# First attention's loop in double steps, with the V transposes in psX and evicted by VectorE

## The reference, cut to what matters

```python
q = (query @ Wq).reshape(b, sq, 32, 16).transpose(0, 2, 1, 3)
k = (key @ Wk).reshape(b, sk, 8, 16).transpose(0, 2, 1, 3)
v = (value @ Wv).reshape(b, sk, 8, 16).transpose(0, 2, 1, 3)
k = jnp.repeat(k, 4, axis=1); v = jnp.repeat(v, 4, axis=1)
scores = jnp.einsum('bhqd,bhkd->bhqk', q, k) * 16 ** (-0.5)
probs = jax.nn.softmax(scores, axis=-1)
out = jnp.einsum('bhqk,bhkd->bhqd', probs, v)
```

## Time and profile before

| what | us |
|---|---|
| median of three runs | 3961.32 |
| span of the profiled execution | 3957.1 |
| the loop `all_batches`, first to last exponential (start) | 104.1 to 1012.1 |
| one batch in the middle of the loop (first maximum unit to the next batch's) | 561.20 to 618.40, 57.20 |
| busy in 561 to 618: TensorE / VectorE / ScalarE / GpSimd | 56.50 / 37.92 / 33.00 / 25.42 |

### The profile page before, as it was taken

One profiled execution on the slowest core, in us unless ns is written; L12 is line 12 of the kernel. 1 busy time (PEld: TensorE's weight loads), 2 busy tenths in 40 slices (PEclk: granted clock), 3 DMA queues, 4 the chain that ended last, 5 costly groups with the idle time before them and its releaser, 6 DMA issues. The chain is left out here.

```text
span 3957.1 us, 74929 instructions
## 1 busy us (share of the span) xinstructions
PE 3617.3 (91%) x32220; PEld 2431.4 (61%) x32220; DVE 2263.6 (57%) x2562; ACT 1538.2 (39%) x2218; POOL 1386.7 (35%) x892
## 2 busy tenths in 40 slices
PE   6999999999768689999999999999999998686888
PEld 4555555555233456887777788887878746333334
DVE  4666666666279832444544444444444416698972
ACT  2555555555177312222222222222222203676740
POOL 3344444431089311111111111111111004497971
PEclk8999999999789889999999999999999999798999
DMA  6455555552223042111111111111111112221220
GB/s 206 127 139 146 143 141 138 152 133 70 67 78 92 1 157 79 40 39 30 47 31 48 31 40 48 40 48 40 48 40 44 71 41 53 73 91 59 95 66 22
DMA packets 229009, 302.18 MB, mean 76 GB/s; under 512 B 68560, under 2 KB 174992, under 8 KB 227392
## 3 DMA queue, kind: packets, MB, share of 16 engines
q1 hardware_dynamic: 228680, 297.40, 25.6%
HBM read 243.77 MB, written 53.10 MB: 75 GB/s over the span
## 5 line engine op out<-in xcount | busy, mean ns | idle before, releaser
L1754 POOL TENSOR_TENSOR D_ctx_lo<-D_ctx_raw,D_ctx_hi 128x1904 fp32r<-128x1904 f32 x64 | 254.7, 3980 | 1294.2 <-ACT D_ctx_hi L1748 1294.2
L762 DVE TENSOR_REDUCE A_mxc<-A_psX 128x2 f32<-128x768 f32 (+2 forms) x512 | 485.5, 984 | 207.5 <-PE A_psX L792 206.5
L1058 ACT ACTIVATE A_probs<-A_psE 128x1024 f32<-128x1024 f32 (+1 forms) x416 | 426.2, 1025 | 318.5 <-PE A_psE L1091 313.4
L1772 ACT ACTIVATE D_V<-D_psY 119x384 f32<-119x384 f32 x224 | 109.8, 490 | 843.0 <-PE D_psY L1839 843.0
L2096 ACT ACTIVATE D_probs<-D_psE 119x2048 f32<-119x2048 f32 x112 | 210.5, 1879 | 414.9 <-PE D_psE L2223 414.9
L1788 DVE TENSOR_REDUCE D_mxc<-D_psE 128x4 f32<-128x1904 f32 (+1 forms) x128 | 242.2, 1892 | 190.8 <-PE D_psE L1858 190.6
L1839 PE MATMUL D_psY<-D_wv_hi,D_ctx_hi 128*119 128x384 f32 (+1 forms) x896 | 314.8, 351 | 16.4 <-DVE D_K_lo L1783 9.0
L2141 DVE TENSOR_TENSOR D_acc<-D_acc,D_probs 119x1024 f32<-119x1024 f32 x96 | 117.6, 1225 | 353.9 <-ACT D_probs L2096 353.9
L2237 PE MATMUL D_psO<-D_probs,D_V 119*32 119x256 f32 (+1 forms) x5376 | 313.3, 381 | 0.0
L1839 PE MATMUL D_psY<-D_wv_hi,D_ctx_lo 128*119 128x384 f32 (+1 forms) x896 | 302.2, 337 | 0.0
L1839 PE MATMUL D_psY<-D_wv_lo,D_ctx_hi 128*119 128x384 f32 (+1 forms) x896 | 301.9, 337 | 0.0
(11 more groups left out here) (366 smaller groups left out, 7770.7 us busy)
## 6 DMA issues: line engine op xcount, KB each, us to landing
D_ctx_raw<-in_ctx SPq DMA_DIRECT2D x48, 952.0 KB, 5.2
A_land<-in_ctx SPq DMA_DIRECT2D x32, 768.0 KB, 5.7
A_land<-in_ctx SPq DMA_DIRECT2D x16, 1024.0 KB, 5.8
E_Bn<-bc_scratch SPq DMA_DIRECT2D x64, 256.0 KB, 3.6
E_Cn<-bc_scratch SPq DMA_DIRECT2D x64, 256.0 KB, 3.4
k_scratch<-A_Khl SPq DMA_DIRECT2D x32, 384.0 KB, 5.4
A_Kst<-k_scratch SPq DMA_DIRECT2D x64, 192.0 KB, 3.6
A_land<-in_ctx SPq DMA_DIRECT2D x16, 642.0 KB, 4.4
```

The source lines that it names most:

```text
L762: nc.vector.tensor_reduce(mxc[:, u % 4, :, u // 4], psX[:, x % 2, :, 0:w], axis=AX_X, op=ALU.max).then_inc(x_free, 1)
L1058: nc.scalar.activation(probs[0:KW[k], n % NPR, :, :].rearrange("p h q -> p (h q)"), psE[0:KW[k], :], ACT.Exp, scale=HD ** -0.5).then_inc(e ...
L1754: nc.gpsimd.tensor_tensor(ctx_lo[c][:, :, 0:w], ctx_raw[c][:, :, 0:w], ctx_hi[c][:, :, 0:w].bitcast(F32), ALU.subtract).then_inc(lo_done[c ...
```

## The change

The loop's unit becomes a double step d (13 in a batch). TensorE's order in one is: scores of the first step, the first maximum unit ("behind"), the weightings of the two steps before (a pair), the other units ("ahead"), scores of the second step, a V transpose if one is due, and one run of 6 or 12 projection passes. At d = 6 the weighting of step 12 stands after the scores of step 13, so that no pair crosses two groups. Other things that move:

- Units are spread three to a double step: those of (j+1, group 0) in d = 6 to 11 (16 = 3+3+3+3+3+1), those of group 1 in d = 12 and d = 0 to 4 of the next batch. `max_rows` comes at d = 5, ahead of the run, and at d = 11, behind it.
- K of chunks 0 and 1 is projected in halves in d = 0 to 3, chunk 2 in d = 4, chunk 3 in d = 5; V of chunks 0 to 2 in halves in d = 6 to 11, chunk 3 in d = 12.
- The V transposes (d = 8, 10, 12, and 0 of the next batch) write psX and take their turn in its two buffers, between the units. VectorE takes them out (`values_out`) in place of ScalarE.
- The reciprocal stands ahead of unit 8 in place of unit 4.
- The queues of SyncE and GpSimd keep their order; what they wait for comes at other times.

```diff
+    RUNS = [("K", 0, HALVES[0]), ("K", 0, HALVES[1]), ("K", 1, HALVES[0]), ("K", 1, HALVES[1]),
+            ("K", 2, range(12)), ("K", 3, range(12)), ("V", 0, HALVES[0]), ("V", 0, HALVES[1]),
+            ("V", 1, HALVES[0]), ("V", 1, HALVES[1]), ("V", 2, HALVES[0]), ("V", 2, HALVES[1]), ("V", 3, range(12))]
+    TURNS = {8: 0, 10: 1, 12: 2, 0: 3}
+    ROWS_FIRST, ROWS_BEHIND = 5, 11
...
+            us = range(min(NU, 3 * max(at, 0)), min(NU, 3 * (at + 1)))
+        units = [("M", b, g, u) for u in us] if b < B else []
+        n = max(1, len(units) // 2)
+        return units[:n], units[n:]
...
+            def values_out(dve, key):
+                b, c = key[1:]
+                x, (t0, nt) = nth_x(key), TILES[c]
+                dve.wait_ge(x_full, x + 1)
+                nc.vector.tensor_copy(V[b % 2][:, t0:t0 + nt, :, 0:HD],
+                                      psX[:, x % 2, 0, 0:P * nt].rearrange("p (j h d) -> p j h d", j=nt, h=H)
+                                      ).then_inc(x_free, 1)
...
+            def turn(pe, key):
+
+                b, c4 = key[1:]
+                x = nth_x(key)
+                pe.wait_ge(y_free, nth_y(("V", b, c4)) + 1)
+                pe.wait_ge(x_free, x - 1)
+                for t in range(TILES[c4][1]):
+                    last = nc.tensor.transpose(psX[:, x % 2, 0, bass.ts(t, P)], VT[:, c4 % 2, bass.ts(t, P)],
+                                               consts["ident"][:, :])
                 last.then_inc(x_full, 1)
...
-                        for n in range(N):
-                            s, k = divmod(n, KT)
-                            to = divmod(s + 1, 2)
-                            units = maxima(k) if to[0] < B else ()
-                            for u in units[:1]:
-                                maximum(pe, *to, u)
-                            scores(n)
-                            for u in units[1:]:
-                                maximum(pe, *to, u)
-                            if n:
-                                weigh(n - 1)
-                            key, passes = projection(s // 2, s % 2, k)
-                            if key:
-                                project(pe, key, passes)
-                            if k == 11 and to[0] < B:
-                                max_rows(pe, *to)
+                        weighed = 0
+                        for j in range(B):
+                            for d in range(TWOS):
+                                n = STEPS * j + 2 * d
+                                behind, ahead = maxima(j, d)
+                                scores(n)
+                                for _, b, g, u in behind:
+                                    maximum(pe, b, g, u)
+                                for e in range(weighed, n):
+                                    weigh(e)
+                                weighed = n
+                                for _, b, g, u in ahead:
+                                    maximum(pe, b, g, u)
+                                scores(n + 1)
+                                if (n + 1) % KT == 0:
+                                    weigh(n)
+                                    weighed = n + 1
+                                if turned(j, d):
+                                    turn(pe, turned(j, d))
+                                if d == ROWS_FIRST:
+                                    max_rows(pe, j, 1)
+                                key, passes = projection(j, d)
+                                if key:
+                                    project(pe, key, passes)
+                                if d == ROWS_BEHIND and j + 1 < B:
+                                    max_rows(pe, j + 1, 0)
+                        weigh(N - 2)
                         weigh(N - 1)
```

More of the change, by code:

```diff
@@ L594, in l0_attention @@
     identr = consts["identr"]
-    K_STEPS = [(0, 3), (3, 3), (6, 3), (9, 3)]
     PASSES = [(c, a, a2) for c in range(DC) for a, a2 in ((0, 0), (0, 1), (1, 0))]
[L598 to L615, removed]
+    TWOS = STEPS // 2
@@ new lines, in l0_attention, with projection @@
+    HALVES = (range(6), range(6, 12))
+    RUNS = [("K", 0, HALVES[0]), ("K", 0, HALVES[1]), ("K", 1, HALVES[0]), ("K", 1, HALVES[1]),
[3 more added lines that the diff above has]
+    ROWS_FIRST, ROWS_BEHIND = 5, 11
+    def projection(j, d):
+        kind, c, passes = RUNS[d]
+        return ((kind, j + 1, c), passes) if j + 1 < B else (None, None)
@@ L617, in l0_attention @@
+    TURN_OF_X = []
+    for j in range(B):
+        for d in range(TWOS):
+            behind, ahead = maxima(j, d)
+            TURN_OF_X += behind + ahead + [key for key in (turned(j, d), rows_of(j, d)) if key]
+    place_x = {key: n for n, key in enumerate(TURN_OF_X)}
     with ExitStack() as stack:
@@ L754, in drain, with read_maximum @@
                 nc.scalar.activation(to, src, ACT.Copy).then_inc(y_free, 1)
[L756 to L764, removed]
+            def read_maximum(dve, link, b, g, u):
+                x, w = nth_x(("M", b, g, u)), CH[u // 4][1]
+                dve.wait_ge(x_full, x + 1)
+                nc.vector.tensor_reduce(mxc[:, u % 4, :, u // 4], psX[:, x % 2, :, 0:w], axis=AX_X, op=ALU.max
+                                        ).then_inc(x_free, 1)
+                if u < NU - 1:
+                    return
+                dve.wait_ge(x_free, x + 1)
                 link(nc.vector.tensor_reduce(nm[:, :, :], mxc[:, :, :, :], axis=AX_X, op=ALU.max, negate=True))
@@ L796, in max_rows @@
             def max_rows(pe, b, g):
-                x = nth_x(b, g, NU)
+                x = nth_x(("R", b, g))
                 pe.wait_ge(x_free, x - 1)
-                pe.wait_ge(mp_ready, x // NX + 1)
+                pe.wait_ge(mp_ready, 1 if first else 2 * b + g)
                 for n in range(4):
@@ L934, in _ @@
                                                     Qhi[:, at, g, :].bitcast(F32), ALU.subtract).then_inc(lo_out, 1)
-                        read_maxima(dve, link, 0, 0)
+                        for u in range(NU):
+                            read_maximum(dve, link, 0, 0, u)
+                        rows_out(dve, 0, 0)
                     @block.tensor
@@ L1045, in sums_out, with exponential @@
                             nc.scalar.activation(OT[:, s % 2, :], psO[:, 0:HQ], ACT.Copy).then_inc(o_copied, 1)
-                        for n in range(N):
+                        def exponential(n):
                             s, k = divmod(n, KT)
[L1049 to L1052, removed]
                             if s and k == 1:
@@ L1059, in _ @@
                                                  psE[0:KW[k], :], ACT.Exp, scale=HD ** -0.5).then_inc(e_free, 1)
+                        for j in range(B):
+                            for d in range(TWOS):
+                                exponential(STEPS * j + 2 * d)
+                                exponential(STEPS * j + 2 * d + 1)
+                                key, passes = projection(j, d)
+                                if key and passes[-1] == len(PASSES) - 1:
+                                    drain(act, key)
                         sums_out(2 * B - 1)
@@ L1085, in scores @@
                             if k == 0 and s:
[L1086 removed]
+                                pe.wait_ge(x_free, nth_x(("R", j, g)) + 1)
                             for pair in range(2):
```

57 lines of the change are left out of this document (47 added, 10 removed).

## The result

The changed kernel takes 4025.69 us (4021.97 to 4029.92, 4 runs) against 3961.85 (3959.71 to 3964.03). The ratio is 1.016, 95% interval 1.0148 to 1.0172. It is slower by 64 us, where 19 were forecast, and lies above the predicted range. The profiled execution's span is 4028.2 us, 71 over the span of before.

The account below looks back on a forecast made before the run. TensorE's own queue was taken to bound the loop. Savings of -3.9 and -1.7 against added waits gave +1.2 us a batch, +17 in 14 middle batches, +19 with the ends: 3980 us, range 3970 to 3995.

Parts of the forecast that it names:

- the wait at unit 8: At group 0's unit 8, d = 8, TensorE waits 2.2 us a batch for chunk 2 of K, landing at 38.7.
- Rival 1: TensorE's clock falls behind the wait in each batch: 1.5 to 2 us a batch, +25, 4005 us; chance 0.16.
- Before and behind it stand dense runs, which the last batch has not: Argument against a clock fall at the 2.2 us wait in each batch; the last batch's window has clock 0.70.
- PEclk under 1.00 inside 200 to 900: Sign that the forecast is wrong: TensorE's granted clock below full speed within that stretch of the loop.
- Its landing 6.5 later: In SyncE's queue, the write of chunk 2 of K lands 6.5 us after 586.19, ahead of four reads.
- the same terms of the forecast: Per batch: -3.9 changes of piece, -1.7 old waits, +0.5 ScalarE, +1.55 transposes, +2.5 units; chunk 2's +2.2 left out.
- the 1.3 of waits at d = 8: VectorE waits at the transpose and unit 9, 0.65 us each, taken as covered by the wait for chunk 2.
- The last batch: Without projections, it alternates two uneven halves where it now overlaps one weighting per step: about +1 us.
- the pair's 0.13 a time: The second weighting of a pair costs 0.43, saving the fixed 0.13: 12 pairs, 1.6 us a batch.
- Transposes as VectorE's waits: Transposes at d = 8, 10, 12, 0 wait for VectorE's read of the first "ahead" unit: together 2.2 us.
- The V copy: On VectorE, taken as 0.5 us for 384 numbers, at no cost since it stands behind the units.
- So this is worth nothing: ScalarE loses four evictions a batch of some 0.5 us each, but TensorE does not wait for it: no gain.

Follow-up runs that it names:

- e5: e4 with both reciprocals moved from ahead of unit 8 to behind unit 15: 3965.05 us, 1.0006 of the kernel before.
- e1: The changed kernel with the context reload in SyncE's queue moved from behind chunk 1 of K to behind chunk 3: 3983.49 us, 1.0058 of the kernel before.
- e3: The kernel before, with the context reload moved behind chunk 3 of K: 3959.45 us, ratio 0.9997.
- e9: e4 with the reciprocal of group 0 ahead of unit 13 and that of group 1 behind unit 15: 3946.20 us, 0.9962 of the kernel before.
- e11: e9 with the last batch in single steps (scores, units, one weighting): 3938.30 us, 0.9944 of the kernel before.
- e4: e1 with the V transposes behind the run of projections in place of ahead of it: 3959.82 us, 0.9995 of the kernel before.
- e2: The changed kernel with 12 extra matmuls of 128x512 ahead of unit 8 of group 0 in each batch: 4013.56 us, 1.0133 of the kernel before.

## Why the prediction was wrong

- **The direction and the wait at unit 8 held.** TensorE waits at unit 8 of group 0 for K of chunk 2, for the reason given. The first four double steps were put at 16.8 us and take 16.9 (593.93 to 610.84), the write of chunk 1 was put at 19.1 and stands at 19.2, unit 8's place without the wait at 36.5 (36.7: 630.6 by the row).
- **The step that failed most is the clock, which the sum put at nothing.** Rival 1 had its mechanism and its price (1.5 to 2 us a batch, "4005") and a chance of 0.16 only. "Before and behind it stand dense runs, which the last batch has not" was the argument against it, and it was wrong: the clock falls in 12 of the 14 batches behind the first, behind waits of 2.0 to 3.8 us among dense runs, and in e5 behind two of 1.2 and 1.07. A fall costs 1.5 us, 2.8 where it lasts twice as long, together some 21 us. PEclk under 1.00 inside 200 to 900 was among the signs of being wrong, and it is 0.97.
- **The wait itself was put too short: 2.2, measured 2.9 in the mean, 10 us in 14 batches.** The prediction carried over the durations of one batch. "Its landing 6.5 later" is 7.2 in the mean (before, the middle batches have 6.0 to 7.3, mean 6.7, and I took the one I was looking at). The write of chunk 1 did not add to it: 5.1 in the batch shown, but 4.2 in the mean, against 4.5. K of chunk 2 is there 39.5 behind the batch's start in place of 38.7.
- **The sum by batch:** forecast +1.2; measured +4.3 (61.53 - 57.19). Without the wait and the fall it would be 57.1, and the same terms of the forecast give 56.15 (57.2 - 3.9 - 1.7 + 0.5 + 1.55 + 2.5). So 1.5 of the missing 3.1 are the clock, 0.7 the wait, and 0.9 lie in the other terms: savings put too high, or waits on VectorE and ScalarE put too low. In the batch shown unit 8's place without the wait is right to 0.2, so most of these 0.9 lie behind unit 8; which term it is stays open. e1 agrees: with the late K and the falls gone a batch is 58.43, that is, 57.1 and the 1.3 of waits at d = 8 that the DMA wait was said to cover.
- **The last batch was put at +1.** From the 65-row scores ahead of it to those at its end it takes 59.6 (1022.73 to 1082.34), where the kernel before takes 50.7 (960.61 to 1011.31) and e3, with the same TensorE order, 48.2. That is some 9 us more, though executions differ there by over 2. In e9 it takes 51.9, and with single steps, in e11, 49.4. In the profiled executions the loop's 69 us are 1 in the first batch (forecast 1), 59 in the 14 middle ones (17) and 9 in the last (1).
- **That the double steps save was right; the waits took more than they save.** e9, with the same double steps and the reload, the transposes and the reciprocals at other places, takes 55.76 a batch, 1.4 under the kernel before.
- **The savings.** A pair takes 0.99 (0.98 forecast), so the pair's 0.13 a time is as forecast. Undoing the pairs costs 1.5 a batch, but by an edit that also adds 12 changes of 0.2, so it does not confirm the 1.6. Transposes as VectorE's waits: 2.2 less 0.65 forecast, 1.6 measured (e4).
- **The V copy** on VectorE took 0.56 (384) and 0.69 (512), 0.5 assumed. No run leaves the copy with ScalarE, so what the move to psX and VectorE gives or costs by itself is not shown.
- **"So this is worth nothing"** for ScalarE's four evictions: nothing here contradicts it; it was not tried alone.

## What to carry to other kernels

When a loop is made denser, work out anew when each transfer is wanted, not only when it is issued: a unit that moved 5 us forward turned a chain of DMAs that had some 4 us to spare into the bound, and one reload at another place in the queue gave back 42 of 64 us. A wait of TensorE costs more than itself if its clock falls behind it. Where a trace of the same kernel shows a fall behind a gap of that size, as the earlier trace rows did here behind 1.77, the fall belongs into the sum and not only among the rivals. And an eviction that moves to another engine brings that engine's order with it: where it stands in the queue mattered (transpose ahead of or behind the run: 24 us; reciprocal of group 0 at unit 8 or 13, and of group 1 at unit 8 or behind 15: 14 us).

## What the runs showed of the hardware

- The write of 384 KB of K (chunk 2) lands 7.2 us after its issue where a reload of 768 KB was issued 0.7 ahead of it on the same queue, and 3.9 where the reload comes later (e1); in the kernel before 6.6 and 3.8 (e3).
- Two waits of 1.19 and 1.07 us, with a pair of weightings ahead of them, were enough for TensorE's clock to go to its 1.2 GHz level in dense code (e5), where single ones of 1.2 at most were not (e4, clock 1.00). The length of a wait alone does not decide: in the changed kernel one of 2.1 us (390.48) had no fall behind it, and one of 2.0 in the next batch had. The Trainium skill says on its page TensorE: Matmul & The Clock Gate, in the section on HAM oscillation, that a wait for a DMA that comes back in each pass of a loop throttles the array each time; the changed kernel agrees, with a fall in 12 of its 14 batches behind the first.
- 12 matmuls of no use in each batch, put into the wait, made the changed kernel 12 us faster (e2).
